# Convolution stage of a two-layer kernel: packed loads in another order, conv3 on 64 rows in quarters

## What is computed

```
h = relu(bn1(conv1x1(x, w1)))                  # 128 -> 64 channels
h = relu(bn2(conv3x3(h, w2, 32 groups)))       # 64 -> 64, two channels a group
x = relu(bn3(conv1x1(h, w3)) + x)              # 64 -> 128
y = window attention(layernorm(x)), windows 7x7, shifted by 3, 8 heads,
    with a relative position bias: a small network (2 -> 256 -> 8) over
    sign(t) * (|t| * a + 1e-6) ** p / b, t = 169 relative places x 2
x = x + y;  x = x + mlp(layernorm(x))          # 128 -> 512 -> 128, gelu
```

## Time and profile before

| | us |
|---|---|
| runs shown (three) | 5086.66, 5091.67, 5092.45 |
| median | 5091.67 |
| profiled execution, its own time | 5094.79 |
| span in its trace | 5093.0 |
| TensorE (PE) busy | 4619.0 (91%) |
| VectorE (DVE) busy | 3638.2 (71%) |
| ScalarE (ACT) busy | 3552.5 (70%) |
| GpSimd (POOL) busy | 2603.1 (51%) |

### The profile page before, as it was taken

The page is one execution under the profiler, slowest core; times in us unless marked ns, Lnnn a source line. Parts: engine busy times, 40 slices in busy tenths (PEclk is TensorE's granted clock), DMA queues, the critical chain, the costliest instruction groups (busy, mean ns, idle before and its releaser), DMA issues.

```text
span 5093.0 us, 197119 instructions
## 1 busy us (share of the span) xinstructions
PE 4619.0 (91%) x73232; PEld 3246.6 (64%) x73232; DVE 3638.2 (71%) x7458; ACT 3552.5 (70%) x5899; POOL 2603.1 (51%) x3504
## 2 busy tenths in 40 slices
PE   2788888599999999999999999999999999999998
PEld 1555655466666666666666666666666666666665
DVE  2233333378888888888888888888888888888886
ACT  0333333377777777777777777777777777777776
POOL 5233333255555555555555555555555555555554
PEclk7899999799999999999999999999999999999999
DMA  2334443100000000000000000000000000000000
GB/s 65 104 123 133 129 132 126 54 24 27 27 27 27 27 27 27 27 27 27 27 27 27 27 27 27 27 27 27 27 27 27 27 27 27 27 27 27 27 27 23
DMA packets 304839, 219.23 MB, mean 43 GB/s; under 512 B 49306, under 2 KB 252010, under 8 KB 304682
## 3 DMA queue, kind: packets, MB, share of 16 engines
q1 hardware_dynamic: 304682, 216.79, 14.4%
HBM read 111.12 MB, written 111.94 MB: 44 GB/s over the span
## 4 chain that ended last, share of the span: by engine, by line
PE 59%; DVE 20%; issue 11%; ACT 5%; SPq 2%; DVEq 1%; POOL 1%; DMA 0%; ACTq 0%; POOLq 0%
DVE xn L1063 8%; PE bank L602 8%; PE bank L683 7%; PE bank L658 6%; PE bank L535 5%; PE bank L594 4%; DVE sc L1038 4%; PE bank L625 4%; PE bank L548 4%; PE bank L674 4%; PE bank L585 3%; PE bank L612 3%; DVE z L1063 3%; ACT L851 2%; PE bank L637 2%
## 5 line engine op out<-in xcount | busy, mean ns | idle before, releaser
L1063 DVE SCALAR_TENSOR_TENSOR xn<-x,lnp 98x128 f32<-98x128 f32 x1024 | 873.5, 912 | 3.7 <-POOL lnp L1133 3.7
L1202 POOL TENSOR_TENSOR res<-x,projb 98x512 f32<-98x512 f32 x256 | 325.9, 1273 | 1014.5 <-DVE x L1080 1014.5
L1220 POOL TENSOR_TENSOR sc<-sc,mx 128x784 f32<-128x784 f32 x512 | 788.6, 1541 | 54.7 <-DVE mx L1044 54.7
L683 PE MATMUL bank<-g,fc_sb 128*128 128x392 f32 x2048 | 784.6, 506 | 0.1
L1038 DVE TENSOR_TENSOR sc<-bank,shared 128x392 f32<-128x392 f32 x1024 | 530.0, 560 | 310.6 <-PE bank L612 310.5
L851 ACT ACTIVATE g<-bank,fc1b 128x392 f32<-128x392 f32 x1024 | 574.7, 586 | 124.6 <-PE bank L676 111.1
L674 PE MATMUL bank<-zt_hi,fc_hi 128*128 128x392 f32 x1024 | 452.1, 441 | 153.8 <-ACT g L851 148.5
L625 PE MATMUL bank<-ident_sb,sc 128*113 128x128 f32 x4096 | 530.9, 273 | 0.3 <-ACT shared L861 0.3
L1133 POOL TENSOR_TENSOR lnp<-st 98x8 f32<-98x8 f32 x777 | 146.2, 217 | 746.8 <-DVE st L916 746.8
L625 PEld LDWEIGHTS bank<-ident_sb,sc 128*113 128x113 f32 x4096 | 515.3, 177 | 2.5 <-ACT shared L861 0.7
L1044 DVE TENSOR_REDUCE mx<-sc 128x16 f32<-128x784 f32 x512 | 496.6, 970 | 18.4
(11 more groups left out here) (103 smaller groups left out, 9185.9 us busy)
## 6 DMA issues: line engine op xcount, KB each, us to landing
x<-x_scratch SPq DMA_DIRECT2D x768, 49.0 KB
out_x<-y SPq DMA_DIRECT2D x672, 49.0 KB
xc_even<-in_x SPq DMA_DIRECT2D x128, 196.0 KB
shared<-in_x SPq DMA_DIRECT2D x128, 196.0 KB
x_scratch<-xc_even SPq DMA_DIRECT2D x128, 196.0 KB
x_scratch<-shared SPq DMA_DIRECT2D x128, 196.0 KB
x<-x_scratch SPq DMA_DIRECT2D x256, 38.5 KB
out_x<-y SPq DMA_DIRECT2D x224, 38.5 KB
```

The source lines that it names most:

```text
L683: mm = nc.tensor.matmul(RC[:, 0:ST], fc2[:, c, :], g[:, c], start=c == 0, stop=c == HC - 1)
L1063: ins = V.scalar_tensor_tensor(dst[:, p, :], src[:, p, :], lnp[:, 7, i, p:p + 1], lnp[:, 8, i, p:p + 1].to_broadcast([PT, C]), ALU.add, AL ...
L1220: P.tensor_tensor(out=s_r, in0=s_r, in1=m_r.to_broadcast([128, 2 * HEADS, N]), op=ALU.subtract).then_inc(sub_done, 1)
```

## The change

It has these parts.

- Parameters are packed on the host: all batch norm values in one array of 128x16 (bn3 as a fourth column), `w3` and `w2` in the form in which SBUF holds them. The `prep` chain computes four columns; two matmuls against ident (`b3_ps`) spread bn3's scale and bias over the partitions, into bank 1. `w3` is scaled on VectorE instead of GpSimd.
- The sync queue loads ident (own semaphore), then the first chunk, then w1, bn, w3, w2 and groupmask, then the other chunks. TensorE transposes the first chunk as soon as ident is there.
- The 19 other loads are issued by ScalarE.
- The position table is held as 128x4 instead of 2x169; two transposes (`tab_ps`) bring it back to two rows. Its steps move to earlier chunks, and the last matmuls stand behind `produce` 5, 6 and 7.
- The clearing of `sc` moves from the end of the opening to its start; GpSimd's clearings of quarter, relb, qt and st move behind `w2`.
- `relb`: 13 rows are issued after each of the first four steps, for one half of the partitions; one copy fills the other half before the last pair but one.
- conv2 writes image m's chunks 2r and 2r + 1 into bank 2m + r, both channel halves of a chunk one below the other in 64 partitions. `h2` so has 64 rows a chunk, and conv3 uses 64 rows in one matmul, without adding up halves. For chunks 2 and 3 the halves are swapped, which a third column of bn2 and the second block of `w3` follow.
- conv3 goes in quarters (image m, chunk pair r); the second image's quarter waits for the sums of the same banks only, and the very first for two of ScalarE's outputs. The order of all engines in a step follows. ScalarE makes the last `h1` ahead of the relus of image 1.

```diff
-CONV_PREP = ["border", "half", "quarter", "relb_clear", "qt_clear", "st_clear",
-             "bn_var", "bn_rstd", "bn_scale", "bn_shift", "bn_bias", "w2",
-             "b3_var", "b3_rstd", "b3_scale", "b3_shift", "b3_bias", "w3"]
+CONV_PREP = ["half", "border", "bn_var", "bn_rstd", "bn_scale", "bn_shift", "bn_bias", "b3_ps", "b3_bias", "w3", "w2",
+             "quarter", "relb_clear", "qt_clear", "st_clear"]
...
+            FIRST_LOADS.append(ident)
+            sp.dma_start(ident[:], a["ident"]).then_inc(first_load, 16)
+            chunk_in(0, 0, ORDER[0])
+            conv_load_in(w1[:], a["w1"])
+            conv_load_in(bn[:].rearrange("p v k -> p (v k)"), a["bn"])
+            conv_load_in(w3[:].rearrange("p k c -> p (k c)"), a["w3"])
+            conv_load_in(staging[:], a["w2"])
             conv_load_in(groupmask[:], a["groupmask"])
...
+            for c in ORDER[1:]:
                 chunk_in(0, 0, c)
...
+            rows = 0
+            for gp in range(2):
+                for s in range(STEPS):
+                    step_out(gp, gp, s)
+                    if rows == 0:
+                        sp.wait_ge(tb_store, 16)
+                    spread_bias(rows, min(rows + 13, N))
+                    rows = min(rows + 13, N)
...
+            sp.wait_ge(tb_load, 16 * N)
+            sp.dma_start(relb[QROWS:QROWS + N], relb[0:N]).then_inc(tb_load, 16)
...
                         for b in range(4):
-                            mm = nc.tensor.matmul(bank[b][HALF * j:HALF * j + HALF, 0:CHT],
+                            m, half_ = divmod(b, 2)
+                            rows = MID * (j % 2) + HALF * (half_ ^ (j // 2))
+                            mm = nc.tensor.matmul(bank[2 * m + j // 2][rows:rows + HALF, 0:CHT],
...
-            def conv3(gp, s, m):
-                pe.wait_ge(h2_sb, first(gp, s, 0) // 2 + 4)
+            def conv3(gp, s, m, r):
+                pe.wait_ge(h2_sb, first(gp, s, 0) // 2 + (2 if m == 0 and r == 0 else 4))
                 if m == 1:
-                    pe.wait_ge(xc_summed, 1 + first(gp, s, 1))
+                    pe.wait_ge(xc_summed, 1 + first(gp, s, 0) + 2 * r + 2)
                 for t in range(TILES):
-                    for half_ in range(2):
-                        for j in range(GROUPS):
-                            mm = nc.tensor.matmul(bank[j][0:CT, C * t:C * t + C],
-                                                  h2[HALF * j:HALF * j + HALF, 2 * m + half_].rearrange(
-                                                      "p (q t) -> p t q", t=TILES)[:, t],
-                                                  w3[HALF * j:HALF * j + HALF, half_],
-                                                  start=half_ == 0, stop=half_ == 1)
+                    for i in range(2):
+                        j = 2 * r + i
+                        mm = nc.tensor.matmul(bank[j][0:CT, C * t:C * t + C],
+                                              h2[MID * i:MID * i + MID, 2 * m + r].rearrange(
+                                                  "p (q t) -> p t q", t=TILES)[:, t],
+                                              w3[MID * i:MID * i + MID, r], start=True, stop=True)
...
                     conv2(gp, u, s)
                     if later(gp, 1):
                         produce(gp + 1, 1 - u, GROUPS * s)
+                    conv3(gp, s, 0, 0)
+                    if later(gp, 1):
                         produce(gp + 1, 1 - u, GROUPS * s + 1)
-                    conv3(gp, s, 0)
+                    conv3(gp, s, 0, 1)
                     if later(gp, 1):
                         produce(gp + 1, 1 - u, GROUPS * s + 2)
-                    conv3(gp, s, 1)
+                    conv3(gp, s, 1, 0)
+                    conv3(gp, s, 1, 1)
                     if later(gp, 1):
                         produce(gp + 1, 1 - u, GROUPS * s + 3)
```

More of the change, by code:

```diff
@@ L171, in program @@
         w3 = sb("w3_sb", [128, 2, C])
[L172 to L175, removed]
+        bn = sb("bn", [128, 4, 4])
+        bn_var, bn_rstd, bn_scale, bn_shift, bn_bias = [sb(f"bn_{i}", [128, 4]) for i in range(5)]
+        b3_bias = sb("b3_bias", [128, C])
         wqkv = sb("wqkv", [C, 3 * C])
@@ new lines, in _, with spread_bias @@
+            sp.dma_start(ident[:], a["ident"]).then_inc(first_load, 16)
[4 more added lines that the diff above has]
+            conv_load_in(staging[:], a["w2"])
+            conv_load_in(groupmask[:], a["groupmask"])
+            for c in ORDER[1:]:
+                chunk_in(0, 0, c)
+            def spread_bias(n0, n1):
+                for n in range(n0, n1):
+                    nj, ni = divmod(n, WIN)
+                    first = REL - 1 - ((nj + WIN - 1) * (2 * WIN - 1) + ni + WIN - 1)
+                    src = bass.AP(tensor=tb_dram.tensor, offset=first,
+                                  ap=[[REL, HEADS], [2 * WIN - 1, WIN], [1, WIN]])
+                    sp.dma_start(relb[n:n + 1], src).then_inc(tb_load, 16)
@@ L477, in bias_steps @@
             def bias_steps(c):
-                if c == 8:
+                if c == 5:
+                    at(pe, "tab_ps")
+                    for i in range(2):
+                        mm = nc.tensor.transpose(bank[0][0:2, 128 * i:128 * i + 128], tab[:, 2 * i:2 * i + 2], ident[:])
+                    mm.then_inc(prep, 1)
+                if c == 6:
                     at(pe, "hidden_ps")
@@ L928, in _ @@
             V.memset(h1[:], 0.0).then_inc(prep, 1)
[L929 to L931 removed]
             def bias_steps(c):
[L935 removed]
+                if c == 0:
+                    at(dve, "b3_bias")
+                    b3_scale_ps = bank[1][:, 0:C].unsqueeze(1).to_broadcast([128, 2, C])
+                    V.tensor_copy(b3_bias[:], bank[1][:, C:2 * C]).then_inc(prep, 1)
+                    step("w3", V.tensor_tensor, out=w3[:], in0=w3[:], in1=b3_scale_ps, op=ALU.mult)
+                    step("w2", V.tensor_tensor, out=w2[:], in0=w2raw,
+                         in1=groupmask[:].unsqueeze(1).to_broadcast([128, TAPS, HALF]), op=ALU.mult)
+                if c == 1:
                     step("positive", V.tensor_scalar, par_pos[:, 0:3], par[:, 0:3], 0.0, None, ALU.max)
```

227 lines of the change are left out of this document (120 added, 107 removed).

## The result

| | us |
|---|---|
| before, runs beside it (four) | 5092.06 (5086.66 to 5092.76) |
| after (four) | **4878.85** (4871.42 to 4881.20) |
| ratio after/before | 0.9581, 95% interval 0.9564 to 0.9598 |
| span of the profiled execution | 5093.0 before, 4878.6 after |

The account below looks back on a forecast made before the run. It took the kernel to be held by a serial opening, a DMA stall and TensorE's waits for sums and `h`; 78.6 + 22 + 96 + 14 + 10 = 221 us off 5094.8 gave 4874, median 4871 us, range 4805 to 4935.

Parts of the forecast that it names:

- The opening: Stretch up to the first conv2: new load order and cheaper powers bring it from 123.6 to 45 us, minus 78.6.
- VectorE's six small steps: about +4 us: In the opening, `prep` adds ScalarE waits after chunk 0, behind GpSimd's clears and these steps, about 4 us in all.
- The stall: TensorE's 24.2 us wait for the third pair's chunks goes once relb rows are spread over four steps, minus 22.
- The steady steps: Convolution stage: conv3 in quarters saves 6.4 us per pair over 15 pairs, minus 96.
- what changes is the order: Steady steps: conv3 rounds stay at 0.18 us; interleaving quarters with `produce` gives 13.1 us instead of 15.65 and 16.99.
- TensorE never waits: Steady steps: sums and ScalarE's `h` end before TensorE needs them, so `produce` 0 to conv2 takes 13.1 us.
- The clock: Conv2 after a pair's end runs at 2.4 GHz, without the idle 2.35 us ahead: minus 14, bounds 0 and 17.
- The last pair: Its two steps, without `produce`, each lose 5.1 us of waits for ScalarE's outputs and the sums, minus 10.
- Rival 1: Conv3 load rounds get shorter because two load streams share what four shared: 61 us more, 4810 us, chance 0.12.
- Rivals 3 and 4: Conv2 row groups sharing a bank take turns, about 5090, chance 0.03; or hold up the queue, about 6600, chance 0.04.
- Rival 2: Steady gain fails through separate conv3 pieces and lost load overlap: 4974 or 4930 us, chance 0.15 together with Rival 5.
- Rival 5: Steps stay bound by a queue; only opening, stall and last pair gain: 4981 us, chance 0.15 together with Rival 2.

Follow-up runs that it names:

- experiment 5: Changed kernel with GpSimd's eight bias additions of the opening all behind the position table's steps: 4875.15 us.
- 10: Changed kernel with contiguous conv3 weights, TensorE's pair loop written out and GpSimd's opening additions behind the position table's steps, all together: 4789.09 us.
- experiment 2: Changed kernel's opening, loads and relb moves, with the old 32-row mapping of conv2 and conv3 and the old step order: 4995.93 us.
- experiment 9: Changed kernel with all 98 rows of relb issued at once behind the table, ahead of the first chunk stores, and without the copy: 4910.45 us.
- Experiment 1: Changed kernel with conv3 kept on 64 rows but in halves, with the old order and the old waits: 4925.19 us.
- experiment 7: Changed kernel with ScalarE's two relu groups of image 1 ahead of the last h1 again: 4905.10 us.
- experiment 8: 64-row kernel in halves and old order, with the chunk-pair loop inside the tile loop, so all four banks of an image finish together: 4969.12 us.
- experiment 3: Changed kernel's order in quarters, but with conv3 on the old 32-row mapping: 5144.96 us.
- experiment 6: Changed kernel with TensorE's loop over pairs written out, without jumps back: 4854.86 us.
- experiment 4: Changed kernel with ScalarE writing h2 sorted by tile, so conv3 loads its 98 weight columns side by side: 4812.18 us.

## Why the prediction was right, and where its terms were not

**The opening: -71.8 instead of -78.6.** The front went as said: the eight issues ended at 4.38 (4.6; eight times 0.45 from 0.74 is in fact 4.3), batch norms done at 10.5 (10), first copy at 12.27 (11.6). ScalarE's 19 loads took not 8.5 or 13 us but until 16.6, up to 1.95 us each:

```profile
13.89 1.95 ACTq L727 DMA_DIRECT2D ln<-in_norm_w  x1
15.87 0.74 ACTq L727 DMA_DIRECT2D ln<-in_norm_b  x1
```

Its first output came at 18.00. That seems to have cost next to nothing: the table's first step on ScalarE, at 19.64, waited 0.96 us more for GpSimd's clearings. The term that was too small is "VectorE's six small steps: about +4 us" together with "they run beside `produce`": GpSimd's additions were costed at nothing, while four of the small steps took 1.7 to 2.3 us beside them, 7.6 us more than alone (experiment 5). The second is TensorE's clock, costed only in the steady stage. Of 38 to 47 us it was busy 8.69 us at a granted clock of 0.50:

```profile
38.00:47.00 9.00, 8.69 (x32) 4.74 (x33) 3.35 (x8) 2.06 (x4) 2.75 (x3) 0.50 0.01 2
```

Nine profiled executions share this opening (after and all experiments but 5 and 10). Two have 0.50 in these 9 us and the first conv2 at 51.8 (after and experiment 2). The other seven have 0.88 to 1.00 and the first conv2 at 46.2 to 47.6. So the 51.79 is that of the slower kind, by about 4 to 6 us, and what the clock does not explain of the 6.8 us missed is 1.2 to 2.6. The small steps are larger than that, since the 4 us allowed for `prep` covered part of them.

**The stall: right**, -22.5 for -22, and experiment 9 puts it back alone. With the steps of now the spread rows are worth 32.

**The steady steps: right in size (-89.6 for -96), incomplete in reason.** The ordinary gaps are 12.82 and 13.05, as worked out (13.1), and TensorE's rounds are unchanged, as argued from the 271 ns. Two things were wrong in the step "what changes is the order". First, most of the gain does not need the quarters between the `produce`. Experiment 1 has the old order and gives 71 of the 117 us (2 against 1), the other 46 come with quarters and ScalarE's order, of which ScalarE's `h1` ahead of the relus is worth 26 where the quarters are there (7). What the 64 rows buy is that a chunk pair needs no second channel half and so finishes in the middle of a half, and VectorE's sums run beside the rest; experiment 8 takes that away and loses 44 us. But on 32 rows the quarters do not gain 46 us, they lose 149 (3 against 2), most of it at the lower clock. Second, the prediction said "TensorE never waits". At each of six jumps back in its loop it waits 1.5 to 2.2 us more. Before, a jump also fell on a pair's end, where TensorE waited 2.35 us for `h`, and the gaps at a jump were 16.9 us like the others; so it seems that the removed wait uncovered it. That is 11 us of gaps, more than the whole shortfall.

**The clock: -18.7 for -14.** It was not the clock alone. conv2 at its best took 7.97 us before and 7.94 after. Before, 14 of the 32 conv2 had a mean granted clock under 1.00, after it 4; at the 1.2 us each of the prediction these ten are an estimated 12 us. "2.4 GHz throughout" holds but for those four. The rest is holes between matmuls, which the prediction did not have: the six conv2 behind a jump took 10.4 to 11.3 us, three of them with the clock at 1.00 throughout. conv2 in sum moved by 12 us in experiment 6 and again in 7, about as much as the gaps did (12 and 14), but experiment 7 shows that this does not all fall behind the longer wait.

**The last pair: right**, -10.8 for -10.

**The rivals.** Rival 1 needed loads near 165 ns; they stayed at 271. The size it gave, 4810, is what experiment 4 reaches by contiguous columns, but by them, not by fewer row groups. Rivals 3 and 4 (one bank, two row groups) fall with conv2 at 7.95 us before and after. The rule of the Trainium skill (TensorEngine Tiling (Array Packing), Restrictions and Gotchas), that different row tiles cannot access one bank at the same time, does not show where they write different groups of 32 partitions. The Trainium skill (PSUM — Partial Sum Buffer, "PSUM bank collisions raise a hardware error") quotes that rule too, but itself keeps accesses apart by bank and group of 32 partitions; with this the trace agrees, at 7.94 us. Rival 2's price, a separate quarter that loses overlap, is 0.19 us a quarter (1.71 against 1.52 us of loads); the sum had it, with 1.65 for such a quarter. Rival 5 had nothing: no wait for `xc`.

## What to carry to other kernels

A matmul that splits its sum over fewer passes may be worth it even where TensorE gets no faster, if it lets some of its banks finish early: look in the timeline at when the next engine starts, not only at the length of the matmuls. Test a new order and a new shape apart and together: here the order gained 46 us with one shape and lost 149 with the other. Before you cost a removed wait in full, ask what else stands at that place and ended earlier, a loop's jump above all. And if weight loads of equal width differ by line, compare the step of their columns: here the fix was one reordered output of ScalarE's at no cost. And look at the start of the first conv2 in more than one execution before you explain a few microseconds of it.

## What the runs showed of the hardware

- A load of 98 fp32 columns takes 271 ns at a step of four elements and 161 side by side, on 64 rows; at the step of four its round is 0.18 us whether two or four row groups take part. The Trainium skill (TensorE: Matmul & The Clock Gate, LDWEIGHTS) has only the number of columns in the price.
- Two row groups that write one bank, in different groups of 32 partitions, cost conv2 nothing: 7.94 us at its best, 7.97 with a bank for each.
- A jump back in TensorE's list costs 1.5 to 2.2 us ahead of the next matmul and about 2 us in holes in the conv2 behind it: 24 us for six jumps. No run here tells what fills them.
- Four of VectorE's steps on 128x3 or 128x4 elements, 0.15 to 0.23 us alone, took 1.7 to 2.3 us beside GpSimd's additions, and each ended with an addition. Copies out of a bank (128x392, about 0.56 us each) were not slowed.
- The granted clock can be 0.50 for 17.8 us in which TensorE was busy 17.66 (experiment 3). What brings this on stays open.
- A DMA issue on ScalarE's queue took 0.31 to 1.95 us in the kernel after, on the sync queue 0.38 to 0.43 for its first eight.
